# First tile of an attention and feed-forward kernel: one batch's probabilities transposed in blocks through DRAM, tile two without TensorE transposes, two weight pieces loaded later

## The chip, the cores and the metric

The kernel runs on one core of a Trainium2 chip. The metric is the device time of one execution in microseconds (us). Before the change three executions took 1515.83, 1516.21 and 1516.26 us; the median is 1516.21 us.

## The reference

Per batch of 256 query tokens (32 batches, 77 context tokens, width 256, 8 heads of 32) the kernel computes a cross attention with a residual and then a gated feed-forward network of width 1024 with a residual:

```python
    x = x + xattn(layernorm(x), ctx)        # q, k, v, masked softmax over 77 keys, attn @ v, Wo
    x = x + ffn(layernorm(x))               # below
    h = silu(tlin(x, w1_w, w1_s)) * tlin(x, w2_w, w2_s)
    h = gelu(tlin(h, h1_w, h1_s), approximate=False)
    h = gelu(tlin(h, h2_w, h2_s), approximate=False)
    return tlin(h, w3_w, w3_s)
```

The feed-forward weights are ternary; `tlin` is a matmul followed by a scale per output feature.

## The kernel before, in words

The tokens are worked in 16 tiles of 512 (two batches each). All engines walk the same list of steps, each taking its own part of a step. The list `FIRST` (line 78) is the opening: tile 0's attention, the keys and values of tiles 2 to 15 ahead of time, tile 1's queries, keys and values, and the loading of all weights. After it come 16 passes over `ORDER` (line 57), in each of which the feed-forward network of one tile runs beside the attention of the next.

The steps that matter here, all of the opening, with the second number of a step as its index:

- `KX` n, `VX` n: TensorE computes keys or values for the later tiles into one of three banks of `ffn_banks` (lines 742, 750, 760). `KD` (ScalarE) and `VD` (VectorE, line 1004) move them to SBUF. A `KX` or `VX` waits until the step three places before it in that series has been moved out, since it takes the same bank.
- `T1`: LN of the tile transposed by eight 128x128 matmuls with an identity (line 632); `Q`, `K`, `V`: query, key, value projections (658, 640, 646); `S`: scores (675).
- `MASK`, `MAX`, `SUB`, `EXP`, `SOFT`: softmax, on VectorE but for `EXP`. Index 0 is the first batch of the tile, 1 the second.
- `PT` 0 to 3: the probabilities transposed by TensorE, eight 128x128 matmuls each (line 691), and copied out to `attn_t` (first batch, `PT` 0 and 1) and `attn_t2` (second batch, 2 and 3). `PV`: probabilities times values (706). `O`: output projection (716). `ADD`: residual on VectorE (1050).
- `LN2S`, `LN2A`, `T2`: the second layer norm's statistics and rows on VectorE (902, 914), transposed on TensorE (725); ScalarE rounds the result to `ln2_hi` (883), VectorE writes the rest to `ln2_lo` (1067). The first feed-forward step `L1` 0 (line 518) waits for `ln2_lo`.
- `CHECK` n: a weight piece of 1 MB is tested for values that its rounded form would not hold; `COUNT` and `FLAG` make one number of the eleven checks; `READ` loads it into a register of TensorE, and a branch on it chooses the loop that follows.
- `KEEP`: SyncE copies each checked piece, SBUF to SBUF, to where the matmuls read it. Its first instruction waits until all eleven pieces have landed. `SPILL`: it writes the later tiles' keys and values to DRAM; the activations of `L1` 3, `L1` 7 and `L2` 0 on ScalarE wait for these writes, because they write over the same SBUF.

In the passes of `ORDER` no transposes of the probabilities run on TensorE. There `DT` transposes 32x32 blocks on VectorE (1035, 1038), and SyncE writes the blocks to DRAM and reads them back in order (`MV`, lines 416 to 431). All transfers are issued by SyncE on one hardware queue, in program order: the eleven pieces are issued by `load_piece` (382) from 6.6 us on.

## Time and profile before

| | |
|---|---|
| median of 3 runs | 1516.21 us |
| the profiled execution, its own time | 1516.25 us |
| its span in the trace | 1514.5 us |
| TensorE matmul busy | 1510.2 us (100%) |
| VectorE busy | 838.6 us (55%) |
| ScalarE busy | 735.6 us (49%) |
| GpSimd busy | 115.0 us (8%) |
| DMA queue of SyncE | 137.47 MB, 30.2% of 16 engines |

Times in the trace count from the start of the span. The span ends with the last instruction; the execution's own time is 1.75 us more. The busy share of TensorE is an upper view, since ends of pipelined matmuls are modelled; the distance from one group's start to the next group's start is what a group costs.

### The profile page before, as it was taken

To read this page: it belongs to the slowest core of one execution; us is meant where nothing else is said; L and a number is where in the kernel's file an instruction comes from. 1 tells how busy PE (TensorE), PEld (TensorE's weight loads), DVE (VectorE), ACT (ScalarE), POOL (GpSimd) and SP (SyncE) were. 2 spreads that over 40 slices of the span, in tenths; PEclk is the share of its full clock that TensorE was granted. 3 is DMA by queue.
4 is the path that set the end of the run, shared out by engine and by line. 5 is a ranking of instruction groups with operands and counts; after the bars stand their busy time and mean duration, and the time that the engine had idled before them with its cause. 6 is when DMAs were issued, how large, how long until landed. Compare 5 with 4: busy or idle time off the path is not lost.

```text
span 1514.5 us, 20501 instructions
## 1 busy us (share of the span) xinstructions
PE 1510.2 (100%) x7802; PEld 1208.6 (80%) x7802; DVE 838.6 (55%) x1320; ACT 735.6 (49%) x1076; POOL 115.0 (8%) x119
## 2 busy tenths in 40 slices
PE   9999999999999999999999999999999999999999
PEld 6787887878878787887878878787887878878888
DVE  6764835547464574745548464574745648364432
ACT  5753635436364453635536354453634536354442
POOL 1001010010100101010010100101001010100000
PEclk9999999999999999999999999999999999999999
DMA  9952322223213323223223312322233223222200
GB/s 370 357 211 70 88 79 62 76 82 97 78 42 99 75 82 78 66 87 76 76 76 93 87 42 76 91 87 78 56 90 83 76 69 92 78 59 69 55 16 15
DMA packets 133185, 137.79 MB, mean 91 GB/s; under 512 B 74018, under 2 KB 105130, under 8 KB 130346
## 3 DMA queue, kind: packets, MB, share of 16 engines
q1 hardware_dynamic: 133162, 137.47, 30.2%
q8 instruction: 15, 0.25, 0.1%
q14 instruction: 8, 0.07, 0.0%
HBM read 77.66 MB, written 48.25 MB: 83 GB/s over the span
## 4 chain that ended last, share of the span: by engine, by line
PE 100%; DMA 0%; SPq 0%; issue 0%
PE ffn_banks L518 85%; PE att_banks L716 4%; PE att_banks L658 4%; PE att_banks L675 2%; PE att_banks L706 2%; PE ffn_banks L760 1%; PE ffn_banks L750 1%; PE ffn_banks L602 1%; PE ffn_banks L742 0%; PE att_banks L691 0%; PE att_banks L646 0%; DMA c_later<-in_ctx_later 0%; PE att_banks L640 0%; PE att_banks L632 0%; PE att_banks L544 0%; PE att_banks L725 0%
## 5 line engine op out<-in xcount | busy, mean ns | idle before, releaser
L518 PE MATMUL ffn_banks<-b_hi,h_sb 128*128 128x512 f32 x1024 | 403.0, 394 | 0.0
L518 PE MATMUL ffn_banks<-b_lo,h_sb 128*128 128x512 f32 x1024 | 398.7, 389 | 0.0
L518 PE MATMUL ffn_banks<-a_hi,h_sb 128*128 128x512 f32 x1024 | 398.3, 389 | 0.0
L518 PE MATMUL ffn_banks<-a_lo,h_sb 128*128 128x512 f32 x1024 | 398.3, 389 | 0.0
L831 ACT ACTIVATE a_f<-ffn_banks,vec 128x512 f32<-128x512 f32 x128 | 88.2, 689 | 367.3 <-PE ffn_banks L518 367.3
L974 DVE TENSOR_TENSOR a_lo<-a_f,a_hi 128x512 fp32r<-128x512 f32 x128 | 103.9, 812 | 273.1 <-ACT a_hi L832 273.0
L518 PEld LDWEIGHTS ffn_banks<-b_hi,h_sb 128*128 128x128 f32 x1024 | 192.2, 188 | 45.6 <-issue 6.2
L518 PEld LDWEIGHTS ffn_banks<-a_hi,h_sb 128*128 128x128 f32 x1024 | 192.2, 188 | 39.9
L518 PEld LDWEIGHTS ffn_banks<-a_lo,h_sb 128*128 128x128 f32 x1024 | 192.2, 188 | 39.9
L518 PEld LDWEIGHTS ffn_banks<-b_lo,h_sb 128*128 128x128 f32 x1024 | 192.3, 188 | 39.4
L518 PE MATMUL ffn_banks<-ln_hi,w_sb 128*128 128x512 f32 x512 | 203.5, 397 | 0.0
L518 PE MATMUL ffn_banks<-ln_lo,w_sb 128*128 128x512 f32 x512 | 200.2, 391 | 0.0
L974 DVE TENSOR_TENSOR b_lo<-b_f,b_hi 128x512 fp32r<-128x512 f32 x128 | 84.6, 680 | 180.0 <-ACT b_hi L832 180.0
L831 ACT ACTIVATE b_f<-ffn_banks,vec 128x512 f32<-128x512 f32 x128 | 88.2, 689 | 178.6 <-PE ffn_banks L518 177.2
L961 DVE SCALAR_TENSOR_TENSOR a_f<-ffn_banks,vec,a_f 128x512 f32<-128x512 f32 x128 | 95.6, 747 | 47.7 <-PE ffn_banks L518 26.8
L809 ACT ACTIVATE a_f<-ffn_banks,vec 128x512 f32<-128x512 f32 x128 | 88.3, 690 | 54.0 <-PE ffn_banks L518 53.8
L518 PEld LDWEIGHTS ffn_banks<-ln_hi,w_sb 128*128 128x128 f32 x512 | 96.0, 188 | 22.6 <-DVE a_f L961 0.2
L518 PEld LDWEIGHTS ffn_banks<-ln_lo,w_sb 128*128 128x128 f32 x512 | 96.2, 188 | 19.8
L518 PE MATMUL ffn_banks<-a_hi,w_sb 128*128 128x512 f32 x240 | 99.1, 413 | 0.0
L966 DVE TENSOR_TENSOR a_lo<-a_f,a_hi 128x512 fp32r<-128x512 f32 x128 | 97.6, 762 | 1.4
L518 PE MATMUL ffn_banks<-a_lo,w_sb 128*128 128x512 f32 x240 | 93.4, 389 | 0.0
L832 ACT ACTIVATE b_hi<-ffn_banks,vec 128x512 fp32r<-128x512 f32 x128 | 87.5, 683 | 0.0
(116 smaller groups left out, 1541.9 us busy)
## 6 DMA issues: line engine op xcount, KB each, us to landing
blocks_dram<-blocks SPq DMA_DIRECT2D x30, 512.0 KB, 3.0
attn_t<-blocks_dram SPq DMA_DIRECT2D x60, 256.0 KB
h_bits<-in_h SPq DMA_DIRECT2D x8, 1024.0 KB, 20.8
h_sb<-h_bits SPq DMA_DIRECT2D x8, 1024.0 KB, 10.6
x_in<-in_x SPq DMA_DIRECT2D x15, 512.0 KB, 3.7
row_blocks_dram<-row_blocks SPq DMA_DIRECT2D x15, 512.0 KB, 4.1
row_blocks<-row_blocks_dram SPq DMA_DIRECT2D x60, 128.0 KB, 3.1
out_rows_dram<-out_blocks SPq DMA_DIRECT2D x120, 64.0 KB, 1.9
```

What stands on the lines that cost most here:

```text
L518: mm = nc.tensor.matmul(psum, left, right, start=(k == 0 and part == 0), stop=(k == rows - 1 and part == 1))
L602: mm = nc.tensor.matmul(fb[:, j, 0:D], rows[:, k, j * P:(j + 1) * P], w3_sb[:, k, :], start=(k == 0 and part == 0), stop=(k == KH - 1 and ...
L658: mm = nc.tensor.matmul(ab[:, m, :], wq_sb[:, k, m * P:(m + 1) * P], ln1_t[:, k, :], start=(k == 0), stop=(k == KD - 1))
L675: mm = nc.tensor.matmul(ab[:, h, at:at + TK], q_t[rows, g, tokens], k_t[rows, g, n * TK:(n + 1) * TK], start=True, stop=True)
L706: mm = nc.tensor.matmul(ab[HD * h:HD * (h + 1), bank, g * TQ:(g + 1) * TQ], v_sb[:, n, (4 * g + h) * HD:(4 * g + h + 1) * HD], probs_t, st ...
L716: mm = nc.tensor.matmul(ab[:, 2 + j // 2, (j % 2) * D:(j % 2 + 1) * D], heads_t[:, k, j * P:(j + 1) * P], wo_sb[:, k, :], start=(k == 0), ...
L809: nc.scalar.activation(a_f32[:, n, :], fb[:, 2 * (n % 2), :], ACT.Silu, scale=s1_sb[:, n:n + 1]).then_inc(silu_done, 1)
L831: nc.scalar.activation(f32[:, n, :], fb[:, n % 4, :], ACT.Gelu, scale=scale[:, n:n + 1])
L832: nc.scalar.activation(hi[:, n, :], fb[:, n % 4, :], ACT.Gelu, scale=scale[:, n:n + 1]).then_inc(done, 1)
L961: nc.vector.scalar_tensor_tensor(out=a_f32[:, n, :], in0=fb[:, 2 * (n % 2) + 1, :], scalar=s2_sb[:, n:n + 1], in1=a_f32[:, n, :], op0=ALU. ...
L966: nc.vector.tensor_tensor(a_lo[:, m, :], a_f32[:, m, :], a_hi[:, m, :].bitcast(F32), ALU.subtract)\
L974: nc.vector.tensor_tensor(lo[:, n, :], f32[:, n, :], hi[:, n, :].bitcast(F32), ALU.subtract).then_inc(done, 1)
```

## The change

In the opening the first batch of tile 0 (`PT` 0 and 1) is no longer transposed on TensorE: `DT` 0 transposes it in blocks on VectorE, and SyncE writes the blocks to DRAM and reads them back, as the passes of the loop do. Tile 1's layer norm is no longer transposed on TensorE (`XLN` and `T1` 0, 1 are gone): SyncE loads x already transposed and the statistics as rows, into the new tile `first_rows`, and VectorE applies them (`LN1A` 0, 1). The new transfers stand in SyncE's program behind piece 8, and the pieces 9 and 10 behind them. `VX` 1, `VX` 6, `FLAG` and `READ` stand elsewhere in the list, and check 8 moves from VectorE to ScalarE. The core of the diff:

```diff
-ACT_CHECKS = (0, 1, 2, 3, 4, 5, 7, 10)
-DVE_CHECKS = (6, 8, 9)
+ACT_CHECKS = (0, 1, 2, 3, 4, 5, 7, 8, 10)
+DVE_CHECKS = (6, 9)
...
+        first_rows, _ = put("first_rows", [P, 2, TILE], at=b_lo_at + 8192)
...
+            def write_blocks(n, done):
+                sp.wait_ge(blocked, done + 1)
+                sp.dma_start(blocks_dram[n], blocks[:]).then_inc(blocks_out, 16)
+                sp.wait_ge(blocked, done + 2)
+                sp.dma_start(tails_dram[n], tail_blocks[:]).then_inc(blocks_out, 16)
+
+            def read_blocks(n, done):
+                sp.wait_ge(blocks_out, 16 * done + 32)
+                dst = (attn_t, attn_t2)[n][:].rearrange("k h q -> k (h q)").rearrange("k (r i) -> k r i", r=4)
+                for c in range(2):
+                    src = blocks_dram[n][:, c, :].rearrange("(r k) i -> k r i", r=4)
+                    sp.dma_start(dst[32 * c:32 * c + 32], src).then_inc(blocks_back[n], 16)
+                part = H * NB * 16
+                for g in range(HG):
+                    src = tails_dram[n].rearrange("(r g k) i -> g k r i", r=4, g=HG)[g, 3:16]
+                    sp.dma_start(dst[64:TK, :, part * g:part * g + part], src).then_inc(blocks_back[n], 16)
...
-            for c in range(3, NP):
+            for c in range(3, NP - 2):
                 load_piece(c)
+            write_rows(1)
+            write_blocks(0, 0)
+            read_blocks(0, 0)
+            load_xt(1)
+            load_rows(1, first_rows)
+            load_piece(NP - 2)
+            load_piece(NP - 1)
             one_pass(None, 0, 1, False)
...
                     if step == "PV":
                         if f is not None:
-                            pe.wait_ge(blocks_back[n], 64 * t)
+                            pe.wait_ge(blocks_back[n], 64 * (t + 1 - n))
                         elif n == 0:
-                            pe.wait_ge(pt_act_done, NQ)
-                            pe.wait_ge(pt_dve_done, NQ)
+                            pe.wait_ge(blocks_back[0], 64)
+                            pe.wait_ge(pt_act_done, 2)
+                            pe.wait_ge(pt_dve_done, 2)
...
-                        dve.wait_ge(t1_ready, 2)
+                        dve.wait_ge(pv_ready, NB)
                         ln_apply(x1, 1, t)
```

SyncE's program behind the first transfers of the opening. Before:

```order
L361 DMA c_later<-in_ctx_later 128x216
L496 DMA w_att_sb<-in_w_att 128x512
L382 DMA h_bits<-in_h 128x2048 x8
L382 DMA w_bits<-in_w 128x2048
L357 DMA ctx_sb<-in_ctx_t 128x308 [waits pv_ready]
```

After:

```order
L401 DMA h_bits<-in_h 128x2048 x7
L350 DMA ln_rows_dram<-ln_stat 128x2x4 [waits ln1_rstd]
L359 DMA blocks_dram<-blocks 128x1024 [waits blocked]
L361 DMA tails_dram<-tail_blocks 128x256 [waits blocked]
L368 DMA attn_t<-blocks_dram 32x4x512 [waits blocks_out]
L368 DMA attn_t<-blocks_dram 32x4x512
L372 DMA attn_t<-tails_dram 13x4x256 x2
L345 DMA ln_t<-in_x_t 128x1024
L355 DMA first_rows<-ln_rows_dram 128x1024 [waits rows_written]
L401 DMA h_bits<-in_h 128x2048
L401 DMA w_bits<-in_w 128x2048
L376 DMA ctx_sb<-in_ctx_t 128x308 [waits pv_ready]
```

Nine transfers now stand between piece 8 and piece 9, the last two pieces behind them.

TensorE's program from `KX` 7 to `PV`. Before (750 and 760 are `KX` and `VX`, 691 is `PT`, 706 is `PV`):

```order
L691 MATMUL att_banks<-id_95,probs 77x128 [waits ln1t_done]
L691 MATMUL att_banks<-id_95,probs 77x128 x7
L750 MATMUL ffn_banks<-c_later,w_att_sb 128x512 [waits later_loaded3,vx_done,kx_done]
L750 MATMUL ffn_banks<-c_later,w_att_sb 128x512
L750 MATMUL ffn_banks<-c_later,w_att_sb 128x108 [waits later_loaded4,vx_done,kx_done]
L750 MATMUL ffn_banks<-c_later,w_att_sb 128x108 x3
L691 MATMUL att_banks<-id_95,probs 77x128 [waits pt_dve_done,pt_act_done,probs_ready]
L691 MATMUL att_banks<-id_95,probs 77x128 x15
L760 MATMUL ffn_banks<-w_att_sb,c_later 128x256 [waits v_w_loaded,later_loaded2,vx_done,kx_done]
L760 MATMUL ffn_banks<-w_att_sb,c_later 128x256 x3
L706 MATMUL att_banks<-attn_t,v_sb 32x256 [waits pt_dve_done,pt_act_done]
```

After (757 and 767 are `KX` and `VX`, 697 is `PT`, 713 is `PV`):

```order
L757 MATMUL ffn_banks<-c_later,w_att_sb 128x512 [waits later_loaded3,vx_done,kx_done]
L757 MATMUL ffn_banks<-c_later,w_att_sb 128x512
L757 MATMUL ffn_banks<-c_later,w_att_sb 128x108 [waits later_loaded4,vx_done,kx_done]
L757 MATMUL ffn_banks<-c_later,w_att_sb 128x108 x3
L767 MATMUL ffn_banks<-w_att_sb,c_later 128x256 [waits v_w_loaded,later_loaded2,vx_done,kx_done]
L767 MATMUL ffn_banks<-w_att_sb,c_later 128x256 x3
L697 MATMUL att_banks<-id_96,probs 77x128 [waits masked,s_copied,probs_ready]
L697 MATMUL att_banks<-id_96,probs 77x128 x15
L767 MATMUL ffn_banks<-w_att_sb,c_later 128x256 [waits v_w_loaded,later_loaded2,vx_done,kx_done]
L767 MATMUL ffn_banks<-w_att_sb,c_later 128x256 x3
L713 MATMUL att_banks<-attn_t,v_sb 32x256 [waits pt_dve_done,pt_act_done,blocks_back0]
L713 MATMUL att_banks<-attn_t,v_sb 32x256 x7
```

`VX` 4 now follows `KX` 8 directly, `VX` 5 stands ahead of `PV`, and `PV` waits for `blocks_back0`.

TensorE's program at the end of the opening, from `V` of tile 1 (646) to the branch. Before (765 is `FLAG`, 725 is `T2`, 768 is `READ`):

```order
L646 MATMUL att_banks<-w_att_sb,ctx_sb 77x256 x4
L760 MATMUL ffn_banks<-w_att_sb,c_later 128x256 [waits v_w_loaded,later_loaded3,vx_done,kx_done]
L760 MATMUL ffn_banks<-w_att_sb,c_later 128x256 x3
L765 MATMUL ffn_banks<-ones,inexact_row 1x1 [waits row_summed]
L725 MATMUL att_banks<-id_95,xln 128x128 [waits q_done,ln2_ready]
L725 MATMUL att_banks<-id_95,xln 128x128 x7
L760 MATMUL ffn_banks<-w_att_sb,c_later 128x256 [waits v_w_loaded,later_loaded3,vx_done,kx_done]
L760 MATMUL ffn_banks<-w_att_sb,c_later 128x256 x3
L768 TENSOR_LOAD flag [waits flag_ready]
L768 ISA x2
L760 MATMUL ffn_banks<-w_att_sb,c_later 108x256 [waits v_w_loaded,later_loaded4,vx_done,kx_done]
L760 MATMUL ffn_banks<-w_att_sb,c_later 108x256
```

After (657 is `V`, 732 is `T2`, 772 is `FLAG`, 775 is `READ`):

```order
L657 MATMUL att_banks<-w_att_sb,ctx_sb 77x256 x4
L732 MATMUL att_banks<-id_96,xln 128x128 [waits q_done,ln2_ready]
L732 MATMUL att_banks<-id_96,xln 128x128 x7
L767 MATMUL ffn_banks<-w_att_sb,c_later 128x256 [waits v_w_loaded,later_loaded3,vx_done,kx_done]
L767 MATMUL ffn_banks<-w_att_sb,c_later 128x256 x3
L772 MATMUL ffn_banks<-ones,inexact_row 1x1 [waits row_summed]
L767 MATMUL ffn_banks<-w_att_sb,c_later 108x256 [waits v_w_loaded,later_loaded4,vx_done,kx_done]
L767 MATMUL ffn_banks<-w_att_sb,c_later 108x256
L775 TENSOR_LOAD flag [waits flag_ready]
L775 ISA x2
L782 COMPARE_AND_BRANCH
```

`VX` 6 no longer stands between `V` and `T2`, the register load stands behind the last matmul of `VX` 8 instead of ahead of it, and the branch follows at once.

## Rows read from the trace of the kernel before

**Rows 1.** Waits of TensorE in the first 140 us: engine, tile, line, total, times, longest.

```profile
PE ffn_banks L544 <- POOL id L1147: 1.6, 1, 1.6
```

**Rows 2.** Timeline of TensorE in the opening: start us, us, engine, line, operation.

```profile
39.65 1.91 PE L691 MATMUL att_banks<-id,probs 128*77 128x128 f32 x16
41.40 1.89 PE L760 MATMUL ffn_banks<-w_att_sb,c_later 128*128 128x256 f32 x8
43.22 1.93 PE L706 MATMUL att_banks<-attn_t,v_sb 77*32 77x256 f32 x32
...
50.37 3.60 PE L658 MATMUL att_banks<-ln_t,w_att_sb 128*128 128x512 f32 x8
...
58.52 1.09 PE L725 MATMUL att_banks<-id,xln 128*128 128x128 f32 x8
59.45 2.76 PE L760 MATMUL ffn_banks<-w_att_sb,c_later 128*128 128x256 f32 x12
61.97 0.50 PE L518 MATMUL ffn_banks<-ln_hi,w_sb 128*128 128x512 f32 x1
```

**Rows 3.** Issue of piece 8, from the timeline of SyncE's queue.

```profile
16.13 2.70 SPq L382 DMA_DIRECT2D h_bits<-in_h  x1
```

**Rows 4.** DMA issues, of piece 8 alone: KB each, us to landing.

```profile
h_bits<-in_h SPq DMA_DIRECT2D x1, 1024.0 KB, 24.8
```

**Rows 5.** DMA issues, the last keys written (issued at 58.9 us).

```profile
k_later_dram<-k_later SPq DMA_DIRECT2D x1, 108.0 KB, 12.8
```

**Rows 6.** A window: its us, busy PE, PEld, DVE, ACT, POOL, PEclk, DMA share, GB/s.

```profile
40.00:42.00 2.00, 2.00 (x18) 1.95 (x17) 1.08 (x2) 1.43 (x4) 0.00 (x0) 1.00 1.00 418
```

**Rows 7.** DMA issues, a write of blocks in the first pass (issued at 89.75 us).

```profile
blocks_dram<-blocks SPq DMA_DIRECT2D x1, 512.0 KB, 2.7
```

**Rows 8.** Timeline of SyncE's queue, the reading back of blocks in that pass.

```profile
99.41 0.79 SPq L427 DMA_DIRECT2D attn_t<-blocks_dram  x2
```

**Rows 9.** Windows over that reading, columns as in Rows 6.

```profile
100.60:103.50 2.90, 2.90 (x14) 2.42 (x13) 0.69 (x1) 1.27 (x2) 0.00 (x0) 1.00 0.92 219
103.50:104.50 1.00, 1.00 (x6) 0.81 (x5) 0.00 (x0) 0.00 (x0) 0.00 (x0) 1.00 0.07 12
```

**Rows 10.** Groups of VectorE by form: busy us, mean ns, idle before.

```profile
L1035 DVE STREAM_TRANSPOSE blocks<-probs 128x512 f32<-128x512 f32 x60 | 39.1, 691 | 2.4
...
L925 DVE TENSOR_TENSOR ln_t<-ln_t,ln_rows 128x1024 f32<-128x1024 f32 x14 | 17.1, 1223 | 5.1 <-DMA ln_rows<-ln_rows_dram 5.0
```

**Rows 11.** Timeline of VectorE, the values moved out beside the softmax.

```profile
34.51 0.68 DVE L1004 TENSOR_TENSOR v_later<-ffn_banks,vec 128x512 f32<-128x512 f32 x1
...
38.21 0.68 DVE L1004 TENSOR_TENSOR v_later<-ffn_banks,vec 128x512 f32<-128x512 f32 x1
```

**Rows 12.** Timeline of VectorE from the residual to the second layer norm's rest.

```profile
50.57 1.23 DVE L1050 TENSOR_TENSOR x<-att_banks,x_in 128x1024 f32<-128x1024 f32 x1 [0.57 <-PE att_banks L716]
...
55.74 1.38 DVE L914 TENSOR_SCALAR xln<-x,mv,rstd 128x256 f32<-128x256 f32 x4
...
59.12 0.14 DVE L956 CAST flag<-ffn_banks 1x1 int32<-1x1 f32 x1
60.69 1.23 DVE L1067 TENSOR_TENSOR ln_lo<-att_banks,ln_hi 128x1024 fp32r<-128x1024 f32 x1 [1.44 <-ACT ln_hi L883]
```

**Rows 13.** DMA issues, the rows of statistics of a later tile.

```profile
ln_rows<-ln_rows_dram SPq DMA_DIRECT2D x14, 512.0 KB, 5.1
```

**Rows 14.** Timeline of SyncE's queue, the first weight pieces kept.

```profile
46.03 1.19 SPq L388 DMA_DIRECT2D w_sb<-w_bits  x2
```

**Rows 15.** Timeline of ScalarE, the silu of `L1` 7 in the first pass.

```profile
78.57 0.69 ACT L809 ACTIVATE a_f<-ffn_banks,vec 128x512 f32<-128x512 f32 x1 [0.62 <-PE ffn_banks L518]
```

**Rows 16.** TensorE by form, first 4 us: us busy, mean ns, idle before.

```profile
L544 PE MATMUL ffn_banks<-id 128*128 128x128 f32 x10 | 2.5, 437 | 1.6 <-POOL id L1147 1.6
```

**Rows 17.** The same from 10 to 62 us.

```profile
L632 PE MATMUL att_banks<-id,xln 128*128 128x128 f32 x16 | 2.1, 272 | 0.0
```

More of the change, by code:

```diff
@@ L413, in one_pass @@
                     if step == "MV":
-                        done = 2 * (NB * (t - 1) + n)
-                        sp.wait_ge(blocked, done + 1)
-                        sp.dma_start(blocks_dram[n], blocks[:]).then_inc(blocks_out, 16)
-                        sp.wait_ge(blocked, done + 2)
-                        sp.dma_start(tails_dram[n], tail_blocks[:]).then_inc(blocks_out, 16)
+                        write_blocks(n, 2 * (NB * (t - 1) + n) + 2)
                         if n == 0:
@@ L422, in one_pass @@
                             sp.wait_ge(stored, 32 * f + 32)
-                        sp.wait_ge(blocks_out, 16 * done + 32)
-                        dst = (attn_t, attn_t2)[n][:].rearrange("k h q -> k (h q)").rearrange("k (r i) -> k r i", r=4)
-                        for c in range(2):
-                            src = blocks_dram[n][:, c, :].rearrange("(r k) i -> k r i", r=4)
-                            sp.dma_start(dst[32 * c:32 * c + 32], src).then_inc(blocks_back[n], 16)
-                        part = H * NB * 16
-                        for g in range(HG):
-                            src = tails_dram[n].rearrange("(r g k) i -> g k r i", r=4, g=HG)[g, 3:16]
-                            sp.dma_start(dst[64:TK, :, part * g:part * g + part], src).then_inc(blocks_back[n], 16)
+                        read_blocks(n, 2 * (NB * (t - 1) + n) + 2)
                     if step == "XW":
@@ L456, in one_pass @@
                         sp.wait_ge(stored, 32 * f + 32)
-                        load_rows(t)
+                        load_rows(t, ln1_rows)
                     if step == "L4":
@@ L704, in one_pass @@
                             for h in range(4):
-                                probs_t = (attn_t, attn_t2)[n][:, 4 * g + h, :] if f is None else by_block[:, g, h]
+                                probs_t = attn_t2[:, 4 * g + h, :] if f is None and n == 1 else by_block[:, g, h]
                                 mm = nc.tensor.matmul(ab[HD * h:HD * (h + 1), bank, g * TQ:(g + 1) * TQ],
@@ L813, in one_pass @@
                         act.wait_ge(x1_done, tile + 1)
+                        if f is None:
+                            act.wait_ge(ln1t_done, 2)
                         if f is not None:
@@ L920, in row @@
                 def row(i):
-                    return ln1_rows[:, i:i + 1, :].broadcast_to([P, KD, TILE])
+                    rows = first_rows if isinstance(a, int) and a == 1 else ln1_rows
+                    return rows[:, i:i + 1, :].broadcast_to([P, KD, TILE])
                 dve.wait_ge(xt_loaded, 16 * (a + 1))
@@ L1038, in one_pass @@
                         nc.vector.transpose(tail_blocks[:], tails).then_inc(blocked, 1)
-                    if step == "PT" and n >= 2:
-                        dve.wait_ge(pt_ready, NQ * t + n + 1)
+                    if step == "PT":
+                        dve.wait_ge(pt_ready, n - 1)
                         q0 = (n % 2) * P
-                        nc.vector.tensor_copy((attn_t, attn_t2)[n // 2][:, 4:8, q0:q0 + P],
-                                              ab[0:TK, (2, 0, 2, 0)[n] + 1, :].rearrange("p (h q) -> p h q", h=4))\
+                        nc.vector.tensor_copy(attn_t2[:, 4:8, q0:q0 + P],
+                                              ab[0:TK, (2, 0)[n % 2] + 1, :].rearrange("p (h q) -> p h q", h=4))\
                             .then_inc(pt_dve_done, 1)
@@ L1080, in one_pass @@
                             ln_stats_of(x_in, 0, t)
-                    if step == "XLN":
-                        dve.wait_ge(t1_ready, t)
-                        ln_apply(x1_keep, 0, t)
                     if step == "LN1A":
```

55 lines of the change are left out of this document (26 added, 29 removed), and 11 rows, old and new, of the table FIRST.

## The prediction

> **What bounds the kernel now.** I read the page first: one engine, TensorE, is busy for nearly the whole span, and the chain that ended last is TensorE throughout. Then its waits in the opening: in 140 us there is one, of 1.6 us, for the identity at the very start [rows 1]. So a microsecond counts only if it is a microsecond of TensorE, and every new wait of TensorE is paid in full. Then the timeline of TensorE [rows 2], read by the distance from one start to the next, since ends are modelled. It gives four marks: `PV` starts at 43.22, `O` ends and tile 1's `Q` starts at 50.37, `T2` starts at 58.52, and the first feed-forward matmul at 61.97. From there on the passes run gapless, and the change edits none of their steps. So the forecast is a forecast of how far the mark 61.97 moves. Last I read the DMA issues, because the change puts a transfer where TensorE had needed none.
>
> **What is removed.** Sixteen transposes of two `PT` steps: sixteen of the same kind take 41.40 - 39.65 = 1.75 us. Eight transposes of `T1`: `T2`, of the same shape, takes 59.45 - 58.52 = 0.93. Together 2.7 us, 0.18% of the time. This is the most that the change can give; the other matmuls are only in another order. `XLN`, and ScalarE's copies of these transposes, go too; both engines have idle time, so I count them at nothing, except that the softmax may come up to 1.4 us earlier.
>
> **The first new wait, before `VX` 4.** `DT` 0 puts three transposes on VectorE behind the first `SOFT`: two at 0.69 [rows 10] and one of half the size, 1.8 us. Behind them in VectorE's queue stand `VD` 2, the second `SOFT` and `VD` 3. `VD` 3 ended at 38.21 + 0.68 = 38.9 [rows 11]; now at 40.7, less up to 1.4, so about 40.0. `VX` 4 takes the bank that `VD` 3 empties. Before, two `PT` steps stood between, and `VX` 4 started at 41.40. Now TensorE comes to it about 43.22 - 2.7 - 1.75 - 1.8 = 37.0 and waits some 3 us. Then follow `VX` 4 (1.8), two `PT` (1.75) and `VX` 5 (1.8), and TensorE is at `PV` at about 45.3, where without any wait it would be at 43.22 - 2.7 + 1.8 = 42.3.
>
> **The second, and longer, at `PV`.** The blocks are ready when `SOFT` 0, which ended at 34.5 [rows 11], and `DT` 0 are done, 36.3 or a little earlier. But the queue still holds pieces: piece 8 was issued at 16.13 [rows 3] and took 24.8 us [rows 4], so it lands at 40.9. That a small transfer does not overtake is shown by the last keys: 108 KB took 12.8 us behind megabytes [rows 5], where 512 KB of blocks on an empty queue took 2.7 [rows 7]. So 640 KB of blocks follow piece 8 at 418 GB/s [rows 6], 1.6 us, and with 0.3 for the small write of statistics ahead of them they have landed at 42.8. Only then does SyncE issue the reads. From that issue to the last data takes from 99.41 [rows 8] to about 103.5 [rows 9], 4.1, and 0.2 until the semaphore: the blocks are back at 47.1 (bounds 46.3 and 48.2). That is later than 45.3, so it decides, and it hides the wait before `VX` 4. `PV` moves from 43.22 to 47.1, **+3.9**. Edits with the same answer: `VX` 1 later, check 8 on ScalarE, `VX` 5 ahead of `PV` lie under this wait.
>
> **From `PV` to `O`** nothing changes in length: `VX` 6 stands where `VX` 5 stood. `O` ends at 54.2. `Q` of tile 1 needs `LN1A`. Its x and rows are issued at about 45; rows take 5.1 [rows 13], so 50.1, and two operations of 1.22 [rows 10] end at 52.5. TensorE comes 1.7 us later, so this costs nothing; if the cover were gone, each microsecond would count.
>
> **From `O` to `T2`.** Before, TensorE needed 58.52 - 50.37 = 8.15 us, with `VX` 6 (1.8) in it. That step is now ahead. What remains, 6.2 us, is shorter than VectorE's chain: residual at 50.57, statistics, check 9, rows ending at 55.74 + 1.38 = 57.12 [rows 12]. That is 6.75 behind the end of `O`, 6.85 with the semaphore. `T2` comes 8.15 - 6.85 = 1.3 us nearer, **-1.3**. Check 9 must have its piece for this. Piece 9 follows the reads (about 46.9), x and rows (1 MB), so it lands near 52.5, and the check is due at about 57.5.
>
> **From `T2` to the first feed-forward matmul.** Before 61.97 - 58.52 = 3.45, set by `ln_lo`, which ended at 60.69 + 1.23 = 61.92 [rows 12]. That chain is unchanged. But `READ` stood before `VX` 8 and now stands behind it, and behind VectorE's cast of the flag, which itself now follows `ln_lo`. So the cast (0.14 [rows 12]), the register load and the branch come on top. No row shows the load. It is at least nothing, and at most the 1.7 us that the eight matmuls of `VX` 7 last, since TensorE ran through `VX` 7 and 8 without a gap with the load between them [rows 2]. The ends are 0.14 and 1.84; no row lies near either, and I take the middle, **+1.0**. The Trainium skill (DMA: Bandwidth & Descriptors, Latency and other measured facts) gives a floor of about 600 ns for a tensor_load; if that is this instruction, the term would be 0.74 and the time 1519.6, an estimate. No run here shows it yet.
>
> **The sum.** 3.9 - 1.3 + 1.0 = +3.6 us. The profiled execution took 1516.25 us (span 1514.5 and 1.75 around it), as much as the median 1516.21. Forecast: 1516.25 + 3.6 = 1519.85, say **1519.8 us**. Its own range, with the bounds of the return (-0.8, +1.1) and of the load (-0.9, +0.8): 1518.1 to 1521.7.
>
> **The cost of the two late pieces.** `KEEP` 0 waits for all pieces. It was issued at 46.03 [rows 14]. Now pieces 9 and 10, x and rows make 3 MB behind the reads: 46.9 + 7.5 = 54.4, 54.7 with landing, 8.7 us later. Everything behind on SyncE moves as far, the network only 3.6. The tightest that I find: the silu of `L1` 7 at 78.57 [rows 15] waits for the last keys, which landed at 58.9 + 12.8 = 71.7 [rows 5]. That becomes 82.2 against 80.4: 1.8 us of cover left, so nothing is charged.
>
> **The rivals.**
> - The blocks are not held by the pieces (the other side: not slower). If they land as on an empty queue, they are there at 36.3 + 2.7 = 39.0 and back at 43.3. Then the bank of `VX` 4 decides, `PV` starts at 45.3, and the sum is 2.1 - 1.3 + 1.0 = +1.8, 1518.1 us. It decides once the blocks are back before 45.3. Against it stands the 12.8 us row. Chance 13%.
> - The network meets the late `KEEP` and `SPILL`. If the queue moves by more than 8.7 + 1.8 = 10.5 us, ScalarE's silu waits, and `L2` 0 behind it. The spills issue slowly and a shift of 12 or 13 us would cost 1.5 to 2.5: about 1522. For it: 9 transfers and 20 us of full queue. Against: SyncE has slack in the spills. Chance 12%.
> - TensorE's clock. The granted clock reads 1.00 in all windows, but 128x128 matmuls right after the first idle time took 437 ns [rows 16] against 272 later [rows 17]; their pace is that of 1.2 GHz against 2.4. The kernel before has no idle time of TensorE after that; the new one has about 3 and 1.8 us close together. If the pace halves again for some 4 us, that adds 2, after both waits 4: 1521.8 to 1523.8. The Trainium skill (TensorE: Matmul & The Clock Gate, Part 1) says that the slow clock is the default and activity releases it, which is this mechanism. The idle times are short, so 10%.
> - No wait at all, the whole saving: 1516.25 - 2.7 = 1513.6. It needs the blocks back at 42.3, before they can be written. 3%.
>
> **How the numbers follow.** The forecast has 62%. What a measurement of this kernel can tell from no change is about 0.2%, 3.0 us, so the border is 1519.2. Of the likeliest case some two thirds lie above it (0.42); clock and late spills lie above it (0.22): slower 0.63. Same has the rest of it, and nearly all of the first rival: 0.33. Even the whole saving is under 0.2%, so faster gets 0.04. The range takes the first rival's lower flank with one microsecond and the smaller clock and spill costs: 1517.3 to 1522.3.
>
> **What would show it.** In the new profile: 24 transposes fewer in the opening; a wait of TensorE for VectorE's move-out before `VX` 4, ending near 40; a wait at `PV` for the transfers, ending near 47.1; blocks written taking 6 us or more to land, not 2.7; `T2` released by VectorE's rows at about 61.1; the first feed-forward matmul at 65.6, behind the cast and the load; the first `KEEP` at about 54.7; no wait in the passes. I am wrong if blocks overtake pieces, if the load is free or much dearer, or if TensorE's matmuls after the waits last longer than before.

## The result and the profile after

The changed kernel took 1523.63 us, median of five executions (1522.45 to 1527.17), against 1516.07 (1515.72 to 1516.26): a ratio of 1.0056, 95% interval 1.0045 to 1.0067. It is slower by 7.6 us. The forecast was 1519.8 with a range up to 1522.3: the sign was right, the size was not, and the spread of 4.7 us is itself new (before: 0.5 in five executions, 1.5 in the fifteen run beside experiment 1). The profiled execution took 1523.63 us, its span is 1521.8.

First the waits of TensorE in the first 200 us of the changed kernel, where the kernel before has one of 1.6 [rows 1]:

```profile
PE att_banks L713 <- DMA attn_t<-tails_dram: 2.4, 1, 2.4
PE ffn_banks L767 <- issue: 1.9, 1, 1.9
PE ffn_banks L558 <- POOL id L1153: 1.6, 1, 1.6
PE ffn_banks L532 <- issue: 1.6, 1, 1.6
PE att_banks L732 <- DVE xln L920: 0.4, 1, 0.4
PE att_banks L643 <- DVE xln L920: 0.2, 1, 0.2
```

Then TensorE's timeline in the opening, the rows that answer to [rows 2]:

```profile
39.90 1.96 PE L767 MATMUL ffn_banks<-w_att_sb,c_later 128*128 128x256 f32 x8 [1.95 <-issue]
41.70 1.91 PE L697 MATMUL att_banks<-id,probs 128*77 128x128 f32 x16
43.45 1.89 PE L767 MATMUL ffn_banks<-w_att_sb,c_later 128*128 128x256 f32 x8
47.78 2.38 PE L713 MATMUL att_banks<-attn_t,v_sb 77*32 77x256 f32 x32 [2.44 <-DMA attn_t<-tails_dram]
50.10 3.18 PE L767 MATMUL ffn_banks<-w_att_sb,c_later 128*128 128x256 f32 x8
53.12 3.62 PE L723 MATMUL att_banks<-w_att_sb,heads_t 128*128 128x256 f32 x16
56.57 3.60 PE L669 MATMUL att_banks<-ln_t,w_att_sb 128*128 128x512 f32 x8
...
63.37 1.09 PE L732 MATMUL att_banks<-id,xln 128*128 128x128 f32 x8 [0.42 <-DVE xln L920]
64.30 1.89 PE L767 MATMUL ffn_banks<-w_att_sb,c_later 128*128 128x256 f32 x8
66.12 0.19 PE L772 MATMUL ffn_banks<-ones,inexact_row 128*1 128x1 f32 x2
66.24 1.11 PE L767 MATMUL ffn_banks<-w_att_sb,c_later 128*108 128x256 f32 x4
68.97 0.47 PE L532 MATMUL ffn_banks<-ln_hi,w_sb 128*128 128x512 f32 x1 [1.61 <-issue]
```

Both forecast waits are there and end where they should, 39.9 and 47.8. The first feed-forward matmul comes at 68.97, 7.0 behind the mark of 61.97. Read mark by mark: `PV` is 4.56 later; from `PV` to the end of `O` it took 8.79 where before it took 7.15 (+1.64); from there to `T2` 6.80 against 8.15 (-1.35); from `T2` to the first feed-forward matmul 5.60 against 3.45 (+2.15). The sum is 7.0, and the span grew by 7.3; a wait of 0.7 that the trace has near the end (below) is in this, and some 0.4 less elsewhere, which I have not followed.

The +1.64 is not a wait. `PV`'s matmuls and those of `VX` 6 behind it (the row at 50.10) only ran longer. Windows over that stretch (us, busy PE, PEld, DVE, ACT, POOL, granted clock, DMA share, GB/s):

```profile
47.80:49.00 1.20, 1.20 (x24) 0.77 (x28) 0.46 (x1) 0.08 (x1) 0.00 (x0) 1.00 1.07 379
49.00:50.00 1.00, 1.00 (x16) 0.20 (x7) 0.00 (x0) 0.50 (x1) 0.00 (x0) 0.56 1.01 377
50.00:51.00 1.00, 1.00 (x6) 0.81 (x3) 0.00 (x0) 0.79 (x2) 0.00 (x0) 0.50 1.04 434
...
52.00:53.00 1.00, 1.00 (x5) 0.85 (x4) 0.97 (x2) 0.91 (x3) 0.00 (x0) 0.73 1.02 426
53.00:54.00 1.00, 1.00 (x7) 0.87 (x6) 1.00 (x2) 1.00 (x1) 0.00 (x0) 1.00 1.00 419
```

The granted clock fell to 0.50, 1.2 instead of 2.4 GHz, from about 49.1 to 52.5. Ahead of it TensorE had stood idle 1.95 and 2.44 us, with 7.9 us between the ends of the two waits. The DMA engines are at a share of 1.00 in the same windows, so contention with the transfers is a rival to read against it.

The end of the opening on VectorE, and the first `KEEP` on SyncE's queue:

```profile
65.54 1.23 DVE L1076 TENSOR_TENSOR ln_lo<-att_banks,ln_hi 128x1024 fp32r<-128x1024 f32 x1 [1.38 <-ACT ln_hi L889]
66.68 0.14 DVE L963 CAST flag<-ffn_banks 1x1 int32<-1x1 f32 x1
```

```profile
56.55 1.20 SPq L407 DMA_DIRECT2D w_sb<-w_bits  x2
```

The cast ends at 66.82 and the first feed-forward matmul starts 2.15 us later, though `ln_lo` was ready by then. `KEEP` 0 is 10.5 us later than before [rows 14]; forecast was 8.7.

### The profile page after: what moved, and what is told of

Same layout as the page of the kernel before. It is cut to its first block, busy times and chain, and to the rows that moved or that the text cites. A ratio compares the mean times of both kernels' runs of the same rounds, so it can differ in the third digit from the quotient of the medians.

```text
span 1521.8 us, 20475 instructions
## 1 busy us (share of the span) xinstructions
PE 1510.7 (99%) x7778; PEld 1207.2 (79%) x7778; DVE 839.5 (55%) x1320; ACT 733.9 (48%) x1073; POOL 114.9 (8%) x119
## 4 chain that ended last, share of the span: by engine, by line
PE 97%; DVE 1%; DMA 1%; issue 0%; ACT 0%; SPq 0%; POOL 0%; POOLq 0%; DVEq 0%
PE ffn_banks L532 84%; PE att_banks L723 4%; PE att_banks L669 3%; PE att_banks L686 2%; PE att_banks L713 2%; PE ffn_banks L616 1%; DMA tails_dram<-tail_blocks 0%; PE ffn_banks L767 0%; PE ffn_banks L749 0%; DMA attn_t<-tails_dram 0%; PE ffn_banks L558 0%; DVE xln L920 0%; ACT junk L797 0%; PE ffn_banks L757 0%; DVE probs L1028 0%
## 5 line engine op out<-in xcount | busy, mean ns | idle before, releaser
L532 PEld LDWEIGHTS ffn_banks<-a_hi,h_sb 128*128 128x128 f32 x1024 | 192.2, 188 | 39.9
L532 PEld LDWEIGHTS ffn_banks<-a_lo,h_sb 128*128 128x128 f32 x1024 | 192.2, 188 | 39.9
```

The source lines that it names most:

```text
L532: mm = nc.tensor.matmul(psum, left, right, start=(k == 0 and part == 0), stop=(k == rows - 1 and part == 1))
```

## The experiments

Three theories stand after this first reading. **A**: the extra is the slow clock (idle TensorE, then matmuls at half pace) and a register load that takes 2.15 us when its flag comes last. **B**: it is contention, the blocks and pieces on the queue. **C**: SyncE's late program meets the passes. "After" below is 1523.63, and ratios are against runs of the kernel before made beside each experiment.

**1. Both waits filled with work.** Matmuls of the identity into a spare bank keep TensorE busy while it would wait.

```diff
                     if step == "PV":
+                        if f is None and n == 0:
+                            spin(20, fb[:, 3])
...
+                    if f is None and (step, n) == ("VX", 4):
+                        spin(16, fb[:, 3])
```

> The changed kernel with matmuls on the identity put into TensorE's two new waits: 16 before VX 4, 20 before PV, into a bank of ffn_banks that nothing uses then (they compute nothing that is read). Nothing else changes, and TensorE has the same work to wait for. Theory (the waits let TensorE's clock fall to 1.2 GHz from 49 to 52.5 us, which costs 1.65 us on top of the waits): the granted clock stays 1.00, PV to O takes 1.87 + 1.8, the median falls from 1523.6 to about 1522.0, and the spread of 4.7 us between the runs shrinks below 1 us. Rival (the matmuls of 47.8 to 53 us are slow because of the DMA traffic beside them, which is the same here): they stay slow, the median stays at 1523.6 and the spread stays.

Measured: 1524.94 (1524.33 to 1525.48), ratio 1.0057 [1.0043, 1.0070]. I had mis-sized the filler: each such matmul is two in the trace, 0.113 us each, so it overshot, `VX` 4 came at 41.92 and `PV` at 51.68. So the median says nothing. Two other things do: the granted clock was 1.00 in every execution, and their spread was 1.15 us instead of 4.7. `PV` with `VX` 6 took 1.86 + 1.83 in that trace, with the DMA share at 0.98 to 1.06 beside them. That speaks against B for this stretch.

**2. The flag early.** `FLAG` directly behind `T2`, VectorE's cast ahead of `ln_lo`, `READ` ahead of `VX` 8.

```diff
-    ("LN2A", 0, 0), ("BIAS", 0, 1), ("VADD", 0, 1), ("COUNT", 0, 0), ("T2", 0, 0),
-    ("VX", 7, 0), ("FLAG", 0, 0), ("VD", 7, 0), ("VX", 8, 0), ("VD", 8, 0), ("READ", 0, 0),
+    ("LN2A", 0, 0), ("BIAS", 0, 1), ("VADD", 0, 1), ("COUNT", 0, 0), ("CAST", 0, 0), ("T2", 0, 0), ("FLAG", 0, 0),
+    ("VX", 7, 0), ("VD", 7, 0), ("READ", 0, 0), ("VX", 8, 0), ("VD", 8, 0),
```

> The changed kernel with FLAG's matmul directly behind T2, VectorE's cast ahead of ln_lo, and READ ahead of VX 8 as in the kernel before. Theory (behind the cast, the register load, the branch and the first instructions behind it take 2.15 us in which TensorE has nothing queued): the first feed-forward matmul follows T2 by 3.5 us and not by 5.6, and the median is 2.0 lower, 1521.6. Rival (the gap ahead of the first feed-forward matmul has another cause, such as the kept pieces w_kept, which come 10 us later than before): the gap stays and the time with it.

Measured: 1524.65 (1522.38 to 1526.16), ratio 1.0052 [1.0038, 1.0066]: no gain. Its trace, of an execution of 1526.16, says why. The first feed-forward matmul does come 3.9 behind `T2`, not 5.6, and the wait of 1.6 is gone. But TensorE waits in the first pass, where the changed kernel doesn't. The two longest waits of the first 200 us, and windows of the clock:

```profile
PE att_banks L713 <- DMA attn_t<-tails_dram: 3.1, 2, 2.1
PE ffn_banks L767 <- issue: 1.9, 1, 1.9
```

```profile
40.00:41.00 1.00, 1.00 (x4) 0.83 (x3) 0.00 (x0) 0.00 (x0) 0.00 (x0) 0.51 0.55 167
...
110.00:120.00 10.00, 7.95 (x49) 4.81 (x48) 1.05 (x2) 2.32 (x4) 0.00 (x0) 0.76 0.33 93
120.00:130.00 10.00, 10.00 (x43) 8.36 (x41) 1.38 (x2) 2.53 (x4) 0.00 (x0) 0.90 0.00 0
```

One of the windows of 1 us inside them:

```profile
117.00:118.00 1.00, 1.00 (x3) 0.81 (x4) 0.00 (x0) 0.53 (x1) 0.00 (x0) 0.50 0.00 0
```

`PV`'s second batch of the first pass started at 115.01, after 2.1 us for its blocks, and the clock fell behind it, to 0.50 until about 121.9. From 115 to 118 the DMA share is 0.00, so here contention can't be what makes TensorE slow. By the granted clock in these windows the low stretch costs some 3.4 us (an estimate); with the wait of 2.1 that is more than the 3.6 us by which the first feed-forward matmul came sooner (65.41).

The trace has another low stretch, in the opening, behind one wait alone:

```profile
39.42 3.17 PE L767 MATMUL ffn_banks<-w_att_sb,c_later 128*128 128x256 f32 x8 [1.94 <-issue]
```

The clock reads 0.51 from 40 to 41, and `VX` 4 takes 2.96 us instead of 1.80. In the changed kernel's trace the wait at the same place (1.95) had no such stretch behind it. It costs nothing here, since TensorE waits at `PV` afterwards, 1.02 instead of 2.44. SyncE issues the blocks of the pass behind all `KEEP` and `SPILL`, so what TensorE wins in the opening it waits for there. That is C, as a second limit.

**3. Four pieces behind the blocks.** If the blocks are only late because they stand behind piece 8, two pieces fewer ahead should bring them early.

```diff
-            for c in range(3, NP - 2):
+            for c in range(3, NP - 4):
                 load_piece(c)
...
-            load_piece(NP - 2)
-            load_piece(NP - 1)
+            for c in range(NP - 4, NP):
+                load_piece(c)
```

> The changed kernel with four pieces (7 to 10) loaded behind the blocks and rows, not two. Theory (the blocks wait in the queue for the pieces ahead, 2.5 us each): the blocks land at about 38.5 and not at 42.3, they are back at 43, TensorE does not wait at PV any more but reaches it at 45.3, only the 2 us wait before VX 4 is left, the clock stays 1.00: 2.5 + 1.65 less, 1519.5. Rival (the write and the reading back are slow by themselves, with their small pieces, whatever stands ahead of them): PV stays near 47.8 and the time at 1523.6. A third possibility is that pieces 7 and 8 now come too late for their checks and the time is given back there.

Measured: 1523.77 (1522.94 to 1524.65), ratio 1.0049 [1.0035, 1.0063]. SyncE's queue and TensorE at `PV`:

```profile
34.91 0.33 SPq L359 DMA_DIRECT2D blocks_dram<-blocks  x1
...
37.91 0.80 SPq L368 DMA_DIRECT2D attn_t<-blocks_dram  x2
```

```profile
44.96 1.93 PE L713 MATMUL att_banks<-attn_t,v_sb 77*32 77x256 f32 x32
```

The blocks land within 3 us instead of 7.1, `PV` does not wait, and comes at 44.96, where the prediction's first rival had put it (45.3). The queue explains the lateness of the blocks. The time of 1519.5 that I expected did not come, because two new waits eat the gain: 1.8 us of `K` of tile 1 for its context, now behind four pieces, and again 2.1 at `PV` of the first pass. With the first of them in it the first feed-forward matmul is still 3.07 sooner, at 65.90. The second gives 2.1 back, and the clock behind it (0.57 to 0.50 from 116 to 119, DMA share 0.00 in the first two of these us) some 1.7, an estimate from the windows.

**4. The kernel before with `READ` behind `VX` 8.** Is the place of the register load dear by itself?

```diff
-    ("VX", 7, 0), ("VD", 7, 0), ("READ", 0, 0), ("VX", 8, 0), ("VD", 8, 0),
+    ("VX", 7, 0), ("VD", 7, 0), ("VX", 8, 0), ("VD", 8, 0), ("READ", 0, 0),
```

> The kernel before with READ behind VX 8 as the only edit. The flag is there early here (59.3 us). Theory (load, branch and fetch of the first instructions take about 2 us, hidden only by matmuls already queued): the load can start when VX 8's last matmul is issued, somewhat before it is done at 61.97, so the first feed-forward matmul starts 0.5 to 2 us later, 1516.6 to 1518. Rival (the load itself is cheap, the changed kernel's gap is from waiting for the late cast or something else late): no change, 1516.1.

Measured: 1515.98 (1515.70 to 1516.24), ratio 0.9999 [0.9990, 1.0008]; the first feed-forward matmul stays 3.45 behind `T2`. The place costs nothing while the flag is there early. (Both marks lie 0.29 nearer here than in the kernel before, from a difference that arises before 24.4 us: marks of two traces are good to about 0.3.) The cost in the changed kernel is that the cast comes behind `ln_lo`, so that the load starts when nothing of TensorE is left to cover it.

**5. The waits filled exactly.** As experiment 1, with 8 and 10 filler matmuls.

```diff
-                            spin(20, fb[:, 3])
+                            spin(10, fb[:, 3])
...
-                        spin(16, fb[:, 3])
+                        spin(8, fb[:, 3])
```

> The changed kernel with 8 and 10 filling matmuls (the first filling had each matmul at half its real length, so it delayed PV by 3.9 us). They compute nothing that is read. Two theories of the time. A (the opening alone decides): TensorE's clock stays at 2.4 GHz, the first feed-forward matmul starts at 67.3 instead of 69.0, and the median is 1522.0. B (SyncE's queue is a second limit: everything behind KEEP 0 comes some 10 us later than before, where the first pass has only 5.6 us of slack, so PV of the first pass waits if the opening gets shorter): the opening is 1.65 shorter, PV of the first pass waits for its blocks, and the median is 1522.7 to 1523.7. Both: spread under 1.2 us.

Measured: 1521.22 (1521.03 to 1522.56), ratio 1.0036 [1.0023, 1.0050]: 2.4 us under the changed kernel, with more work on TensorE. Its timeline behind the fillers:

```profile
44.55 2.39 PE L558 MATMUL ffn_banks<-id 128*128 128x128 f32 x20
47.71 1.93 PE L715 MATMUL att_banks<-attn_t,v_sb 77*32 77x256 f32 x32 [0.77 <-DMA attn_t<-tails_dram]
49.58 1.99 PE L771 MATMUL ffn_banks<-w_att_sb,c_later 128*128 128x256 f32 x8
51.41 3.62 PE L725 MATMUL att_banks<-w_att_sb,heads_t 128*128 128x256 f32 x16
```

`PV` starts as before, 47.71 against 47.78, at the end of the same transfer; only what follows is faster, `O` starts at 51.41 and not at 53.12. The clock read 1.00 in every execution, and the transfers beside it are as dense as in the changed kernel:

```profile
50.00:51.00 1.00, 1.00 (x7) 0.87 (x6) 0.00 (x0) 1.00 (x2) 0.00 (x0) 1.00 0.99 393
```

This shows that the +1.64 is the clock's, and that idle time of TensorE causes it. The spread fits: it was 1.5 here, and in the changed kernel the two slowest executions have the lowest mean clock (0.998 against 0.999). The first feed-forward matmul is at 67.31, 1.66 earlier; the other 0.7 of the 2.4 is the wait near the end, which this trace does not have. So theory A's mark came true, and its time of 1522.0 was missed by 0.8, nearly all of it that wait; B's wait at `PV` of the first pass did not come.

**6. Both repairs, and `KEEP` sooner.** Experiments 2 and 5 together, and the lines that make `KEEP` 0 wait for all eleven pieces removed (each copy still waits for the check of its own piece).

```diff
                     if step == "KEEP":
-                        if n == 0:
-                            for c in range(NP):
-                                sp.wait_ge(piece_loaded[c], 16)
                         for c in KEPT[n]:
```

> The changed kernel with three edits: the same filling; FLAG, cast and READ early as in e2; and KEEP 0 without its wait for all eleven pieces (each copy still waits for the check of its own piece), so that SyncE issues the copies at about 51 and not at 56.5, right behind the pieces in the queue. Theory B: the idle 2 us of the queue ahead of KEEP 0 are gone, everything behind comes 2 us sooner or more, and PV of the first pass waits by so much less: about 1520.5 (first feed-forward matmul at 65.2, blocks of the first pass back some 2 us earlier than in e2). Rival A (opening alone): 1519.3. Rival (the copies are slow by themselves and the queue gains nothing): 1522.5 or more.

Measured: 1519.89 (1519.32 to 1520.47), ratio 1.0024 [1.0015, 1.0034]. The first feed-forward matmul is at 65.74, no wait is left in the first pass, `KEEP` 0 is issued at 50.04. The time lies between theory B's 1520.5 and rival A's 1519.3, so this run alone doesn't part them; experiment 9 does it by one edit.

**7. The second part of the change alone.** The kernel before with only tile 1's first layer norm loaded as rows (no `T1` of tile 1) and pieces 9 and 10 behind; all probabilities transposed on TensorE.

```diff
-    ("SUB", 1, 0), ("T1", 0, 1), ("KX", 6, 0), ("EXP", 1, 0), ("KD", 6, 0), ("CHECK", 2, 0), ("VX", 2, 0), ("BIAS", 0, 0),
+    ("SUB", 1, 0), ("KX", 6, 0), ("EXP", 1, 0), ("KD", 6, 0), ("CHECK", 2, 0), ("VX", 2, 0), ("BIAS", 0, 0),
...
-            for c in range(3, NP):
+            for c in range(3, NP - 2):
                 load_piece(c)
+            write_rows(1)
+            sp.wait_ge(q_ready, HG)
+            load_xt(1)
+            load_rows(1, first_rows)
+            load_piece(NP - 2)
+            load_piece(NP - 1)
```

> One part of the change alone, on the kernel before: tile 1's T1 and XLN replaced by x and rows from DRAM and LN1A, with the pieces 9 and 10 behind them; the probabilities are transposed by TensorE as before. It takes eight transposes (0.9 us) from TensorE and puts 1 MB (2.5 us) on a queue with 5.6 us of slack. Theory B: no wait appears, 1516.1 - 0.9 = 1515.2, and the gain is whole; the blocks are what costs. Rival (pieces 9 and 10 behind other transfers are by themselves the harm, through KEEP 0 and its followers): a wait in the first pass, 1516.1 or slower.

Measured: 1517.15 (1516.31 to 1517.51), ratio 1.0007 [0.9998, 1.0016]. Eight transposes less gained nothing. All waits of TensorE in its trace:

```profile
PE ffn_banks L552 <- POOL id L1153: 1.6, 1, 1.6
PE ffn_banks L526 <- DVE a_f L967: 0.7, 1, 0.7
PE ffn_banks L753 <- ACT k_later L801: 0.3, 1, 0.3
PE ffn_banks L768 <- DVE inexact_row L958: 0.3, 1, 0.3
```

`T1` had covered a wait: `KX` 6 comes only 0.4 sooner (29.73 against 30.14), since it waits for ScalarE, whose `KD` 3 stood behind `EXP` 0. Then `FLAG` waits for VectorE's row of the checks, and the first feed-forward matmul is at 62.02, no nearer than before (61.97). And there is a wait of 0.7 near 1357 us, taken up below. By difference the rest of the change, the blocks together with the steps that were moved (the register load among them), costs 1523.63 - 1517.15 = 6.5 us.

**8. Three pieces behind, no filling.** Three pieces behind the blocks, `VD` 3 ahead of the second `SOFT`, flag early as in experiment 2, `KEEP` sooner as in experiment 6.

```diff
-    ("SOFT", 0, 0), ("DT", 0, 0), ("VD", 2, 0), ("VX", 3, 0), ("SOFT", 1, 0), ("VD", 3, 0), ("CHECK", 3, 0), ("KX", 7, 0), ("KX", 8, 0),
+    ("SOFT", 0, 0), ("DT", 0, 0), ("VD", 2, 0), ("VX", 3, 0), ("VD", 3, 0), ("SOFT", 1, 0), ("CHECK", 3, 0), ("KX", 7, 0), ("KX", 8, 0),
...
-            for c in range(3, NP - 2):
+            for c in range(3, NP - 3):
                 load_piece(c)
```

> The changed kernel with three pieces behind the blocks, VD 3 ahead of the second SOFT, FLAG and READ early, KEEP 0 without its wait for all pieces, no filling. The opening should have no wait above 1.5 us: blocks back at about 44.5, first feed-forward matmul at 62 to 62.5, about as in the kernel before. Theory B: the queue is then the only limit; PV of the first pass waits for its blocks until about 112 to 113 instead of running at 109 to 110, and the time is 1518.5 to 1520. Rival A (opening alone): 1516.3.

Measured: 1519.48 (1518.96 to 1522.00), ratio 1.0025 [1.0014, 1.0035]. `VX` 4 has no wait (37.63), `PV` waits 1.9 and starts at 45.24, the context costs 0.9, the first feed-forward matmul is at 63.91. The clock held in the traced execution (1519.26); in five of the other seven the mean clock reads 0.999 or 0.998, so it fell in some. The time lies in the range that I expected, but by luck: I had put the loss at `PV` of the first pass, which runs at 110.35 without a wait, and had the opening free of waits above 1.5 us and ending at 62 to 62.5. It is the best version with blocks, and still 3.4 us above the kernel before.

**9. Experiment 6 with `KEEP` waiting again.** It isolates the second limit.

```diff
                     if step == "KEEP":
+                        if n == 0:
+                            for c in range(NP):
+                                sp.wait_ge(piece_loaded[c], 16)
```

> This is the version with FLAG and READ early and the two waits filled (1519.89), with one edit taken back: KEEP 0 waits for all eleven pieces again, so SyncE issues it near 56.4 and not 50.0. Theory A, that SyncE's late program is a second limit in the first pass: the blocks of the first pass come back 2.5 us later, 114.8 or so, while TensorE reaches PV of that pass near 112.3; it waits about 2 us there, the granted clock falls behind the wait, and the time is 1522 to 1523.5. Theory B, that SyncE's program has slack enough in the pass and the gain of that version came from the opening alone: no wait at PV of the pass, 1519.5 to 1520.3.

Measured: 1520.50 (1520.14 to 1521.41), ratio 1.0032 [1.0020, 1.0044]: 0.6 above experiment 6, with intervals that overlap; the trace says more. TensorE in the first pass:

```profile
113.67 1.07 PE L715 MATMUL att_banks<-attn_t,v_sb 77*32 77x256 f32 x16 [0.74 <-DMA attn_t<-tails_dram]
```

The wait is there and gone in experiment 6, so the limit exists; it is 0.7 and not the 2 us that theory A expected, and with 0.7 the clock holds. In experiment 2 the same wait was 2.1 and the clock fell. The same transfers ended 1.3 us later there, and the queue's timeline shows where: the issue of the two reads took 2.22 us, not 0.79. Experiment 2, then experiment 9:

```profile
108.88 2.22 SPq L368 DMA_DIRECT2D attn_t<-blocks_dram  x2
```

```profile
108.43 0.79 SPq L368 DMA_DIRECT2D attn_t<-blocks_dram  x2
```

In experiment 3 it took 1.76. Why it is longer in some executions stays open.

**10. The changed kernel with `KEEP` sooner alone.** Only the edit shown under experiment 6.

> The changed kernel with one edit: KEEP 0 does not wait for all eleven pieces, each piece's copy waits only for its own piece. KEEP 0 is issued near 50 and not 56.5. In the changed kernel TensorE reaches PV of the first pass at 115.4 without a wait, so by theory A (the second limit binds only when the opening gets shorter) nothing is gained: 1522.5 to 1524.5, with first feed-forward matmul at 69. Theory B, that KEEP's lateness already costs in the changed kernel: 1521 or less.

Measured: 1523.51 (1521.79 to 1524.57), ratio 1.0048 [1.0034, 1.0062]. `KEEP` 0 is issued at 50.09 and nothing is gained: the first feed-forward matmul is at 68.95, `PV` of the first pass at 115.29, as in the changed kernel (68.97 and 115.31). In the changed kernel itself SyncE's lateness costs nothing; it only stands behind the next microsecond that is won.

**11. Experiment 7 with its two waits taken away.** `KD` 3 ahead of `EXP` 0, `FLAG` behind `T2`.

```diff
-    ("EXP", 0, 0), ("KD", 3, 0),
+    ("KD", 3, 0), ("EXP", 0, 0),
...
-    ("COUNT", 0, 0), ("VX", 6, 0), ("VD", 6, 0), ("FLAG", 0, 0), ("T2", 0, 0),
+    ("COUNT", 0, 0), ("VX", 6, 0), ("VD", 6, 0), ("T2", 0, 0), ("FLAG", 0, 0),
```

> The version with only the second part of the change (tile 1's first layer norm from rows, no T1 of tile 1) ran 1517.15, no faster than before, though eight transposes are gone. Two new waits were in its trace: 0.3 of TensorE before KX 6 for ScalarE's KD 3, which stood behind EXP 0, and 0.3 before FLAG for VectorE's row of the checks, which stands ahead of T2. Here KD 3 is put ahead of EXP 0 and FLAG behind T2. If these two waits ate the saving, the first feed-forward matmul comes near 61.4 instead of 62.0 and the time is 1515.6 to 1516.4. If EXP 0, now later, holds the softmax and PT 0 up, or ln_lo moves with VectorE's late residual, the mark stays at 62.0 and the time at 1517.

Measured: 1518.82 (1517.95 to 1520.25), ratio 1.0020 [1.0011, 1.0030]: slower, by neither of the two ways that I had written down. `T2` did come at 57.52, 1.0 nearer than before. But with `FLAG` its cast moved behind `ln_lo`:

```profile
59.64 1.23 DVE L1073 TENSOR_TENSOR ln_lo<-att_banks,ln_hi 128x1024 fp32r<-128x1024 f32 x1 [1.12 <-ACT ln_hi L888]
60.78 0.14 DVE L962 CAST flag<-ffn_banks 1x1 int32<-1x1 f32 x1
```

```profile
62.69 1.09 PE L763 MATMUL ffn_banks<-w_att_sb,c_later 128*108 128x256 f32 x4 [2.09 <-issue]
```

Cast over at 60.92, next matmul at 62.69: the load takes 1.8 us of an empty TensorE. The clock fell behind this wait as well, to 0.50 in the window from 64 to 66. It seems not to have fallen in every execution: the four with a mean clock of 0.999 took 1519.62 to 1520.25, the six with 1.000 took 1517.95 to 1519.05.

**12. The same with the cast ahead of `ln_lo`.** One edit more; `CAST` is the name of VectorE's part of `FLAG`.

```diff
-    ("COUNT", 0, 0), ("VX", 6, 0), ("VD", 6, 0), ("T2", 0, 0), ("FLAG", 0, 0),
+    ("COUNT", 0, 0), ("CAST", 0, 0), ("VX", 6, 0), ("VD", 6, 0), ("T2", 0, 0), ("FLAG", 0, 0),
```

> The version without T1 of tile 1, with KD 3 ahead of EXP 0 and FLAG behind T2, ran 1518.82; its trace had T2 at 57.5, 1.0 nearer than in the kernel before, and then a wait of 2.1 us at the register load, because VectorE's cast of the flag had come behind ln_lo. One edit more here: the cast stands ahead of ln_lo, with FLAG's matmul still behind T2. If the late cast is what the register load costs, the wait goes, the first feed-forward matmul comes 3.5 to 3.9 behind T2, near 61.2, and the time is 1515.3 to 1516.4. If the load itself is dear wherever it stands, a wait of 1 us or more stays and the time is above 1517.

Measured: 1517.04 (1515.73 to 1517.46), ratio 1.0006 [0.9997, 1.0015]. The wait is gone, 1.8 us are back in the median (the wait of 2.1, and the clock where it fell), and the first feed-forward matmul is at 61.22, 0.75 earlier than in the kernel before. The late cast is what the load costs: shown a second time, in a kernel without blocks. Yet the time does not fall below that of before, and the span, 1514.8, is 0.3 above it. Of this 1.05 one wait near 1357 us takes 0.74; the remaining 0.3 I have not followed:

```profile
1352.46 2.52 DVE L972 TENSOR_TENSOR a_lo<-a_f,a_hi 128x512 fp32r<-128x512 f32 x1
...
1357.05 0.50 PE L526 MATMUL ffn_banks<-ln_hi,w_sb 128*128 128x512 f32 x1 [0.74 <-DVE a_f L967]
```

No version beats the kernel before by an amount that can be measured.

## Why the prediction was wrong, point by point

- **The waits: right.** "The first new wait, before `VX` 4" was forecast to end near 40.0 and ended at 39.90. "The second, and longer, at `PV`" was forecast to 47.1; TensorE started at 47.78. The blocks landed at 42.3 (forecast 42.8); the way back took 5.4 and not 4.3. The term +3.9 measured +4.56, inside its bounds. The reason given, a queue in order, held in experiment 3.
- **"From `PV` to `O` nothing changes in length": wrong.** This is the clock, which I had among the rivals with 10% and a price of +2 to +4, and not in the sum. It cost 1.64 in the traced execution. The argument that "the idle times are short" was the fault: [rows 16, 17] had shown matmuls at about half pace behind idle time (a pace only; the granted clock reads 1.00 there), and I had no row that showed idle times of 2 us to be harmless. The length of a wait does not decide alone. Single waits of 1.94 (experiment 2, in the opening), 2.05 (the same, first pass), 2.15 (experiment 3, first pass) and 2.09 (experiment 11) had the low clock behind them. Waits of 1.95 before `VX` 4, in the changed kernel and in experiment 3, of 1.9 in the traced execution of experiment 8, of 1.6 at the register load and of 0.7 in experiment 9 had not. The runs show no threshold. The rule that I had cited (the Trainium skill, TensorE: Matmul & The Clock Gate, Part 1: slow is the default, activity releases it) agrees with the traces in so far as the clock fell behind idle time only and was back at 1.00 while TensorE worked, in the changed kernel from 52.5 us on.
- **"From `O` to `T2`": right,** -1.35 against -1.3. `LN1A` ended at 54.03, later than the forecast 52.5, and under the cover named.
- **"From `T2` to the first feed-forward matmul": mis-sized,** +2.15 against +1.0, and even above my upper bound of 1.84. The bound was taken from `VX` 7, through which TensorE ran without a gap. Experiment 4 shows what is wrong with such a bound: how much of a load hides under queued matmuls says little of what it takes behind an empty engine. Between the cast's end and the next matmul lie 1.8 us (experiment 11), with the branch 2.15. The floor of about 600 ns that the Trainium skill gives for a tensor_load (DMA: Bandwidth & Descriptors, Latency and other measured facts) is only a floor: the measurement is three times that, and it decides.
- **The late pieces: right in what they cost, wrong in the place.** "Nothing is charged" held for the changed kernel (experiment 10). `KEEP` 0 was 10.5 us later, not 8.7, because piece 10 landed at 56.4, not 54.7. The tightest place is not the silu that I named but `PV` of the first pass. In the changed kernel it starts at 115.31 without a wait; when TensorE comes 3.5 us sooner, at 111.85, its second half waits 0.7 (experiment 9).
- **The sum.** 3.6 + 0.7 (return) + 1.6 (clock) + 1.15 (load) = 7.05, less 0.05 at `T2`: the 7.0 that the mark moved. The failed step is the pair clock and load: the slower stretch behind the waits, left out of the sum (1.64 measured), and the register load, put at +1.0 (2.15 measured). They are 2.8 of the 3.4 us by which the mark was missed, the return most of the rest. Without the 1.64 the median would lie inside the range (1521.99), without the 1.15 just outside it (1522.48). The median was missed by 3.8; beyond the mark there is the wait of 0.7 near the end, told below, which the sum did not have either, and some 0.4 less that I have not followed.
- **The saving.** The 2.7 us are gone from the trace as forecast (24 matmuls fewer), but the 0.93 of `T1` were no gain even alone: experiment 7 shows a wait under it that the kernel before had hidden.

## What to carry to other kernels

A new wait of a TensorE that was never idle can cost more than its length: price it with the stretch at the lower clock that may stand behind it (1.6 to 3.4 us here), and expect the time to spread from run to run; where a wait can't be avoided, cheap matmuls in it can pay for themselves. A register load and its branch can be free while they stand behind work and their operand is early; ask which instruction produces the operand, and what stands ahead of that on its engine, not where the load stands. Removing work from the bounding engine uncovers what the work was hiding, so count the next limit in each queue before counting the saving.
